# Attention block with a quantised side branch on one core: value products in two bursts, an opening that projects batch 2 early

## What is computed

```python
xn = layernorm(x)                                   # no weights
k, q, v = split(xn @ Wqkv + bqkv)                   # 16 heads of 16
scores = einsum('bsnh,btnh->bnst', k, q) / 4
scores = triu(scores) - 10000 * tril(ones, k=-1)
attn = softmax(scores, axis=2)
attn_out = einsum('bnkq,bknh->bqnh', attn, v) @ Wo + bo
x_fp8 = clip(xn / s, -448, 448).astype(float8_e4m3)  # s: input scale
ffn_out = (x_fp8 * s) @ (w_fp8 * w_scale).T
out = x + attn_out + ffn_out
```

## Time and profile before

| what | us |
|---|---|
| median of 3 executions | 215.1 (211.27 to 216.66) |
| the profiled execution: its own time | 213.12 |
| its span, first to last instruction | 211.4 |
| PE busy | 184.2 (87%) |
| DVE busy | 158.8 (75%) |
| POOL busy | 116.2 (55%) |
| ACT busy | 97.0 (46%) |

### The profile page before, as it was taken

The page is one execution under the profiler, slowest core; times in us unless marked ns, Lnnn a source line. Parts: engine busy times, 40 slices in busy tenths (PEclk is TensorE's granted clock), DMA queues, the critical chain, the costliest instruction groups (busy, mean ns, idle before and its releaser), DMA issues.

```text
span 211.4 us, 4667 instructions
## 1 busy us (share of the span) xinstructions
PE 184.2 (87%) x1677; PEld 137.4 (65%) x1677; DVE 158.8 (75%) x342; ACT 97.0 (46%) x169; POOL 116.2 (55%) x207
## 2 busy tenths in 40 slices
PE   4697564699979999999999999999999997997892
PEld 4586353567657677767776777777776764764561
DVE  2778979966778798969796979597959777970451
ACT  2514221236346633763366436643655455348510
POOL 6810600079963795369636973597359737635410
PEclk9999978569999999999999999999999999999998
DMA  5799986302610370137013621352136210001002
GB/s 178 171 333 207 210 203 184 72 2 79 175 51 7 102 200 6 56 88 201 22 50 81 168 60 53 81 150 80 54 81 167 63 50 2 3 5 50 3 3 99
DMA packets 23673, 20.35 MB, mean 96 GB/s; under 512 B 2547, under 2 KB 23395, under 8 KB 23651
## 3 DMA queue, kind: packets, MB, share of 16 engines
q1 hardware_dynamic: 23651, 20.06, 36.4%
HBM read 3.48 MB, written 2.10 MB: 26 GB/s over the span
## 4 chain that ended last, share of the span: by engine, by line
PE 66%; DVE 10%; SPq 9%; issue 5%; ACT 4%; DMA 3%; POOL 2%; ACTq 0%
PE pso L976 8%; PE bankB L1001 8%; SPq L356 7%; PE bankA L1001 7%; PE bankA L1063 6%; PE bankB L1009 5%; PE ps L951 5%; PE ps L956 4%; PE ps L928 3%; PE ps L930 2%; PE bankB L1030 2%; DVE o_masked L758 2%; DVE row_max L721 2%; PE pso L982 2%; PE bankB L1041 2%
## 5 line engine op out<-in xcount | busy, mean ns | idle before, releaser
L460 POOL TENSOR_SCALAR_AFFINE_SELECT probs<-probs 128x256 f32<-128x256 f32 x128 | 52.0, 436 | 70.1 <-ACT probs L525 70.1
L525 ACT ACTIVATE probs<-ps 128x1024 f32<-128x1024 f32 x48 | 49.1, 1025 | 37.2 <-PE ps L951 32.1
L721 DVE TENSOR_REDUCE row_max<-ps 128x4 f32<-128x1024 f32 (+1 forms) x48 | 58.1, 1216 | 2.4 <-PE ps L930 1.3
L951 PE MATMUL ps<-q_stack,k_stack 99*128 99x256 bf16 x128 | 20.0, 281 | 2.9 <-DMA q_stack<-max_rows 2.6
L976 PE MATMUL pso<-probs,v_sb 128*32 128x256 f32 x256 | 20.9, 398 | 0.5 <-POOL probs L460 0.3
L928 PE MATMUL ps<-k_stack,q_stack 96*128 96x128 bf16 x128 | 19.1, 226 | 2.0 <-DVE row_max L721 1.9
L1001 PE MATMUL bankB<-xT,wqk_sb 128*128 128x256 f32 x64 | 18.4, 438 | 1.7 <-ACT xT L575 1.7
L930 PE MATMUL ps<-k_stack,q_stack 125*128 125x128 bf16 x128 | 19.0, 225 | 0.0
L1001 PE MATMUL bankA<-xT,wqk_sb 128*128 128x256 f32 x64 | 16.8, 407 | 0.0
L1001 PEld LDWEIGHTS bankB<-xT,wqk_sb 128*128 128x128 f32 x64 | 13.2, 217 | 4.5 <-ACT xT L575 1.3
L1009 PE MATMUL bankB<-wqkv_sb,xT 128*128 128x256 f32 x64 | 15.3, 382 | 0.3 <-DVE q_rest L746 0.3
(11 more groups left out here) (130 smaller groups left out, 351.3 us busy)
## 6 DMA issues: line engine op xcount, KB each, us to landing
q_stack<-q_parts SPq DMA_DIRECT2D x48, 128.0 KB
k_stack<-k_parts SPq DMA_DIRECT2D x48, 128.0 KB
out_dram<-y SPq DMA_DIRECT2D x8, 256.0 KB, 2.1
x_all<-in_L_attn_x_dram SPq DMA_DIRECT2D x1, 1536.0 KB, 9.9
k_stack<-fixed_k SPq DMA_DIRECT2D x3, 256.0 KB
q_stack<-fixed_q SPq DMA_DIRECT2D x3, 256.0 KB
x_all<-in_L_attn_x_dram SPq DMA_DIRECT2D x2, 256.0 KB, 3.0
wqkv_sb<-in_L_attn_Wqkv_dram SPq DMA_DIRECT2D x1, 512.0 KB, 4.3
```

The source lines that it names most:

```text
L460: ins = pool.affine_select(out=v[:, lo:lo + 2], in_=v[:, lo:lo + 2], compare_op=ALU.is_ge, fill=0.0, base=0, pattern=[[0, 2], [1, P]], cha ...
L525: act.activation(probs[:, i % 2, :], ps[:], ACT.Exp, scale=SCALE).then_inc(exp_done, 1)
L721: dve.tensor_reduce(dst, src, AX_X, ALU.max).then_inc(max_done, 1)
L951: mm = pe.matmul(ps[:, h * S:h * S + S], k_stack[0:K_SOFT, b % STACKS, hh, 0:P], q_stack[0:K_SOFT, b % STACKS, hh, :], start=True, stop=True)
```

## The change

- Warm-up: 13 fp32 products instead of 18 transposes.
- x is loaded in four groups: batch 0, batch 1, batches 2 and 3, batches 4 to 7. The last is issued in step -1 behind the maxima rows, and so are the fixed rows of stack 2. Its statistics are taken in step 0 behind maximum 4, its square roots at the end of ACT's step 0, inverse_std(3) in step 1.
- Batch 2 is transposed and projected (q, k) in PE's step -1 between the maxima blocks of batch 0, v of batch 1 too; ACT does their copies before its steps, POOL splits batch 2 before its steps, SP lays it out in step 0. Step 0 no longer does this.
- On DVE, the magnitude half of clip_x becomes magnitude_x. In step 0 only that half stays for batch 0, in the later steps it moves behind maximum 2. fp8_weight and bv_T move into step -1 behind maximum 4, PE's weight transposes and bias product behind its last maxima block; the masked-key counts move into step 0.
- values: slots 0 to 2 of batch n are run together in slot 3 of step n, slots 3 to 5 together in slot 0 of step n+1 (the last batch keeps its order). probs has six slots, and exponentials waits for the value product six slots back. project_v stands before transpose_o, o_out(n, 0) behind values_out.
- split's subtraction, round_x and residual work in two pieces of 256 elements (split's for DVE too).

```diff
...
-USES_BEFORE = {"A": [("k", 0), ("k", 1)], "B": [("xT", 0), ("q", 0), ("xT", 1), ("q", 1), ("v", 0)]}
+USES_BEFORE = {"A": [("k", 0), ("k", 1), ("k", 2)],
+               "B": [("xT", 0), ("q", 0), ("xT", 1), ("q", 1), ("v", 0), ("xT", 2), ("q", 2), ("v", 1)]}
 FIRST, LAST = -1, B + 1
...
-        probs = sb("probs", [P, 2, 1024])
+        probs = sb("probs", [P, SLOTS, 1024])
...
-        WARM_UP = 18
+        WARM_UP = 13
         NEG = 4
         CONSTS = 3
-        X_GROUPS = ((0, TB), (TB, 2 * TB), (2 * TB, B * TB))
+        X_GROUPS = ((0, TB), (TB, 2 * TB), (2 * TB, 4 * TB), (4 * TB, B * TB))
...
             wait(eng, part2_ready, 2 * b + j + 1)
-            eng.tensor_tensor(pt[:, par, 2], r[:], pt[:, par, 1], ALU.subtract).then_inc(split_ready, 1)
+            for k in range(KT):
+                ins = eng.tensor_tensor(pt[:, par, 2, k], r[:, k], pt[:, par, 1, k], ALU.subtract)
+            ins.then_inc(split_ready, 1)
...
                     to_stack(n + 2)
+                if st.like == 0:
+                    to_stack(2)
                 if st.has(1):
                     max_to_stack(n + 1, 1 - p, 0)
+                if st.like == FIRST:
+                    load_x(3)
+                    fixed_in_stack(2)
             to_stack(1)
-            fixed_in_stack(2)
             all_steps(sp, run)
...
                 wait(pool, quant_dve, 4 * b + 4)
-                pool.tensor_tensor(x_sum[:], x_clip[:, par], x_big[:, par], ALU.add).then_inc(quant_pool, 1)
+                wait(pool, quant_pool, 2 * b)
+                for k in range(KT):
+                    ins = pool.tensor_tensor(x_sum[:, k], x_clip[:, par, k], x_big[:, par, k], ALU.add)
+                ins.then_inc(quant_pool, 1)
                 wait(pool, quant_pool, 2 * b + 1)
                 wait(pool, ffn_mm, b - 1)
-                pool.tensor_tensor(xq[:, par], x_sum[:], x_big[:, par], ALU.subtract).then_inc(quant_pool, 1)
+                for k in range(KT):
+                    ins = pool.tensor_tensor(xq[:, par, k], x_sum[:, k], x_big[:, par, k], ALU.subtract)
+                ins.then_inc(quant_pool, 1)
                 wait(pool, y1_ready, b)
-                pool.tensor_tensor(xb[:], x_all[:, TB * b:TB * b + TB, :],
-                                   out_bias[:].unsqueeze(1).to_broadcast([P, TB, D]),
-                                   ALU.add).then_inc(xb_ready, 1)
+                for g, (lo, _) in enumerate(X_GROUPS):
+                    if lo == TB * b:
+                        pool.wait_ge(x_landed[g], 16)
+                for t in range(TB):
+                    ins = pool.tensor_tensor(xb[:, t], x_all[:, TB * b + t, :], out_bias[:], ALU.add)
+                ins.then_inc(xb_ready, 1)
...
                         pool.wait_ge(out_bias_ready, 1)
-                        for g in range(3):
-                            pool.wait_ge(x_landed[g], 16)
                         residual(0)
...
             pool.wait_ge(split_ready, 2)
-            for qk in "qk":
-                split(pool, 1, 1, qk)
+            for b in range(1, 3):
+                for qk in "qk":
+                    split(pool, b, b % 2, qk)
             all_steps(pool, run)
...
                 act.wait_ge(ph2_mm, c + 1)
-                wait(act, pv_mm, c - 1)
+                wait(act, pv_mm, c - SLOTS + 1)
                 ps = ps1 if st.like == B - 1 and i % 2 else ps2
-                act.activation(probs[:, i % 2, :], ps[:], ACT.Exp, scale=SCALE).then_inc(exp_done, 1)
+                act.activation(probs[:, i, :], ps[:], ACT.Exp, scale=SCALE).then_inc(exp_done, 1)
...
                     exponentials(st, n, 3)
-                    o_out(n, 0)
                 if st.does("v"):
                 if st.has(0):
+                    o_out(n, 0)
                     exponentials(st, n, 4)
...
                     max_out(n + 1, 1 - p, 1, None)
+                if st.like == 0:
+                    square_roots(3)
...
                 part1(b, b, "k", "A")
+            square_roots(2)
             act.wait_ge(v_ones_ready, 1)
             values_out(0, 0)
-            square_roots(2)
+            xT_out(2, 0)
+            part1(2, 0, "q", "B")
+            part1(2, 0, "k", "A")
+            values_out(1, 1)
             all_steps(act, run)
...
                 dve.tensor_scalar(x_clip[:, par], x_over[:], -FP8_MAX, None, ALU.max).then_inc(quant_dve, 1)
+            def magnitude_x(b, par):
                 dve.wait_ge(quant_dve, 4 * b + 2)
...
                                   ALU.mult).then_inc(masked_ready, 1)
+            def count_masked_keys():
+                dve.wait_ge(const_ready, CONSTS)
+                link(dve.tensor_reduce(row_number[:], later[:], AX_X, ALU.add))
+                for t in range(TB):
+                    ins = dve.tensor_scalar(masked_keys[:, t:t + 1], row_number[:], -1.0, float(S - 1 - P * t), ALU.mult, ALU.add)
+                link(ins)
...
                     dve.tensor_tensor(out_bias[:], pso[:, 1, 0], bo_all[:], ALU.add).then_inc(out_bias_ready, 1)
-                    clip_x(0, 0)
+                    magnitude_x(0, 0)
+                    count_masked_keys()
                 if st.has(1):
                     maxima(st, n + 1, 1)
+                if st.like == FIRST:
+                    rest1(2, 0, "q", "B")
                 if st.has(1) and FIRST < st.like < EARLY:
...
                     clip_x(n + 1, 1 - p)
+                if st.has(1) and FIRST < st.like:
+                    magnitude_x(n + 1, 1 - p)
                 if st.does("xT"):
                     negate_and_split(n + 1, 0)
+                if st.like == FIRST:
+                    rest1(2, 0, "k", "A")
                 if st.has(-1):
...
                     maxima(st, n + 1, 4)
+                if st.like == FIRST:
+                    fp8_weight()
+                    dve.wait_ge(bias_mm, 1)
+                    dve.tensor_copy(bv_T[:], pso[:, 0, 0].rearrange("p (k m) -> p k m", k=KT)).then_inc(bv_T_ready, 1)
+                if st.like == 0:
+                    dve.wait_ge(x_landed[3], 16)
+                    link(moments(*X_GROUPS[3]))
+                    variances(3)
                 if st.has(0):
                     maxima(st, n + 1, 5)
-                if st.like == FIRST:
-                    inverse_std(2)
-                    normalise(2, 0)
+                if st.like == 1:
+                    inverse_std(3)
                 if st.like == EARLY:
...
             dve.wait_ge(bqk_col_ready, 1)
-            at, last = X_GROUPS[2]
             rest1(0, 0, "q", "B")
             split(dve, 0, 0, "k")
+            rest1(1, 1, "q", "B")
             dve.wait_ge(x_landed[2], 16)
-            moments(at, at + 5)
-            rest1(1, 1, "q", "B")
-            moments(at + 5, at + 8)
+            link(moments(*X_GROUPS[2]))
+            variances(2)
             rest1(1, 1, "k", "A")
-            fp8_weight()
-            dve.wait_ge(bias_mm, 1)
-            dve.tensor_copy(bv_T[:], pso[:, 0, 0].rearrange("p (k m) -> p k m", k=KT)).then_inc(bv_T_ready, 1)
-            link(moments(at + 8, last))
-            variances(2)
...
+            clip_x(0, 0)
+            inverse_std(2)
+            normalise(2, 0)
             dve.wait_ge(floor_ready, 1)
...
+            def transpose_w8():
...
             def bias_product():
...
             for _ in range(WARM_UP):
-                pe.transpose(ps1[:, 0:P], ident[:], ident[:])
+                pe.matmul(ps1[:, 0:P], ident[:], ident[:], start=True, stop=True)
             transpose_x(None, 0, 0)
...
-            pe.wait_ge(w8_ready, 1)
...
             pe.wait_ge(const_ready, CONSTS)
...
                         phase1(st, n + 1, 1 - p, i)
-                        if st.like == FIRST and i == 1:
-                            bias_product()
+                        if st.like == FIRST:
+                            if i == 0:
+                                transpose_x(None, 2, 0)
+                            elif i == 1:
+                                project_qk(None, 2, 0, "q", "B")
+                            elif i == 2:
+                                project_qk(None, 2, 0, "k", "A")
+                            elif i == 3:
+                                project_v(None, 1, 1)
+                            elif i == 5:
+                                transpose_w8()
+                                bias_product()
                         if i == (4 if st.like == FIRST else 5):
...
                             phase2(st, n, p, j)
-                    if i > 0 and st.has(0):
+                    if i > 0 and st.like == B - 1:
                         values(st, n, p, i - 1)
                     if i == 0 and st.has(-1):
-                        values(st, n - 1, 1 - p, SLOTS - 1)
+                        for j in range(SLOTS // 2, SLOTS):
+                            values(st, n - 1, 1 - p, j)
                     if i == 0:
...
                     elif i == 3:
+                        if st.does("v"):
```

(6 more changed lines are left out.)

23 lines of the change are left out of this document (10 added, 13 removed).

## The result

The kernel after the change takes 215.63 us (median of 4 runs, 215.11 to 216.31), the kernel before, run beside it on the same chip, 213.19 (210.97 to 216.66): ratio 1.0147, 95% interval 1.0099 to 1.0194. Forecast were 207 us, a range of 201 to 213, and faster with a chance of 0.77. The time is outside the range and on the other side of no change, though by less than 2%. Medians here are over all executions; the ratios leave out those, met with many of the kernels, that ran over 1.5% longer than the shortest of the same kernel. The profiled executions stand 2.0 us apart: 215.11 for 213.12, spans 213.4 for 211.4.

The account below looks back on a forecast made before the run. PE was taken to bound the plain steps and DVE step -1. The terms -2.3 (to step 1's start), -5.0 (bursts), +0.8 (table loads), -0.2 (steps 6 to 8) gave 206.4 us profiled, 208.3 median; said 207, range 201 to 213.

Parts of the forecast that it names:

- Warm-up: Opening: 13 fp32 products raise the clock for batch 0's q and k; k_parts of batch 0 comes 2.2 us earlier.
- I add up to 25.2: End of the opening: DVE's first maximum begins at 25.2 us for 28.82, -3.6.
- 8.1 + 1.8 + 1.5 + 1.8 - 0.6: Step -1 on DVE: old time, both rests, fp8_weight and bv_T, q_rest's wait, less old idle: 12.6 us, +4.5.
- fourth term: Step -1: new DVE wait for q_rest, behind transpose, copy, product and ACT, some 1.8 us.
- fifth: Step -1: DVE's old idle time of 0.6 us goes, -0.6.
- a term of 1.2 us for both steps: Steps -1 and 0: low clock costs 0 to 10 us; the half case was taken, +1.2.
- I keep 2.0: Step 0: of 6.2 us in which DVE was not busy 2.0 stay; with 17.5 busy, 19.5 for 23.8, -4.3.
- 0.7 + 0.47 + 0.2 - 0.35 = 1.0 a step: Steps 1 to 5: fewer groups, k_rest's wait gone, o_masked in time, less the wait for maximum 2; -5.0 in all.
- Table loads, +0.8: End of ACT's step 0: two table loads for group 3's square roots push xT of batch 3, +0.8 us.
- The opening gives nothing: Rival: statistics and projections only move, DVE ends step 0 as late as before; 208.7 us, chance 0.17.
- The slow rival: Steps -1 and 0: PE at 1.2 GHz, DVE waits for q, +9.3 for +1.2; 214.5 or 216.5 us, chance 0.07.
- The rival of the DVE-bound plain step: Plain steps: DVE becomes the bound, bursts give nothing, PE waits for maximum 2 and o_masked; 211.4 us, chance 0.17.

Follow-up runs that it names:

- after_filled: Kernel after the change, with products that nothing reads in PE's holes of the opening, step -1 and step 0: 214.19 us, ratio 1.0024.
- proj_only: Kernel after the change, with x in three groups again, all statistics before the maxima, early projections and new warm-up kept: 214.15 us, ratio 1.0058.
- bursts_256: Kernel after the change with its whole opening undone (bursts, mended order and POOL pieces on the kernel before): 210.75 us, ratio 0.9893.
- groups_only: bursts_256 plus x in four groups with the late stack rows and statistics, no early projections, old warm-up: 210.43 us, ratio 0.9875.
- after_512: Kernel after the change with POOL's pieces of 256 undone (split, round_x, residual whole again): 217.43 us, ratio 1.0192.
- before_bursts: Kernel before, with bursts, six probs slots and mended order, POOL whole, opening as before: 210.84 us, ratio 0.9875.

## Why the prediction was wrong, step by step

**Warm-up: right in the mechanism, worth nothing.** The q product of batch 0 took 1.97 us, as foreseen, with 5.0 us for the warm-up (forecast 3.2 to 6.1). But the clock is lost again in the next hole: 0.71 in 16:18, and the q product of batch 1 takes 3.05 us where it took 1.97. The forecast used the gain for batch 0 and took batch 1 as before; it looked for the next hole only behind 22 us.

**First maximum, "I add up to 25.2": 27.36.** The transfer did land earlier than foreseen, but DVE's queue ran late. It had waited 2.21 us for q_parts of batch 1 at 20.07, behind the product of 3.05 us, and has no gap to speak of from there on. The list behind k_rest of batch 1 (clip, inverse_std, normalise) was put at 2.7 us and took 3.5 (23.88 to 27.36). Small instructions were undersized in it: variances and inverse_std(2) have single instructions of 0.42, 0.47 and 0.59 us while POOL splits batch 1, where the shortest of their kind take 0.16.

**Step -1, "8.1 + 1.8 + 1.5 + 1.8 - 0.6": 15.00. Its fourth term failed by 1.5 us and its fifth by 0.9.** DVE's busy time grew by 3.2 (10.65 for 7.45), within 0.1 of what was added. The new wait for q_rest was set at 1.8, worked out with a product of 1.97 us; at the low clock it is 3.33. And "the old idle of 0.6 goes" was wrong: DVE waits 0.93 for maximum 1, since PE runs the transposes of batch 2 ahead of that block. The price of the low clock had been named ("q and k cost 1.8 us more each (3.75 for 1.97) and DVE waits for them") and was taken by half, in a term of 1.2 us for both steps. With the clock held high (after_filled) the step still took 14.0, with waits of 0.89 and 2.32: undersized by 1.4 us even at 2.4 GHz, less what the products that nothing reads take themselves.

**Step 0, 17.5 busy and "I keep 2.0": 18.31 and 3.3.** This is the step that misled most: that PE, losing 7 to 8 us of products, would free the step down to DVE's 17.5. DVE was indeed the bound, but then only its own work could shorten the step, and by the forecast's own count that hardly fell (17.64 to 17.5). What was left to gain were 6.2 us not busy, of which 3.3 stayed: 0.80 for the next block behind the transposes of w8, 1.18 for the ffn product, and 1.0 at the step's end for transpose_o (L1076), which gives o_sum. The PE work ahead of the second and in the third ran at 1.2 GHz (0.50 in 52:54 and 62:64). PE for its part stood still for 3.59 us before 61.97, waiting for o_masked, which stood behind the statistics in DVE's queue. The eight tiles of statistics are DVE work put into a step bound by DVE: with them step 0 is 2.6 us longer (21.60 for 18.99 in proj_only), for a first maximum that comes 1.8 us earlier.

**Bursts, "0.7 + 0.47 + 0.2 - 0.35 = 1.0 a step": 0.46 in step 3 (21.05 for 21.51), 1.5 us over steps 2 to 5.** The groups gave 0.51 of busy time, not 0.7, and the wait for k_rest of 0.47 did go. What failed is the sum: it treated the saving on PE and the waits as independent. PE's saving reaches the step's length only as far as DVE is ready, and the term of 0.2 for o_masked coming in time had the wrong sign (0.19 became 0.39, and 0.78 without the pieces), as DVE's whole queue moved later in the step. The forecast did name maximum 2 as the new wait (0.28 for the 0.35 said). For the groups, the Trainium skill (TensorEngine Tiling (Array Packing), Key Properties) says that a change of tiling mode drains the engine; the rows agree that a change costs something, 0.51 us over the four groups that went. For the pieces, "L755 would wait at most one half piece, -0.4" came out at 0.43 for 0.84 us; that the negate group would land beside POOL was not foreseen. The bursts also shorten step 0, by 1.2 us in bursts_256, which the forecast left out; so against a kernel with bursts and the old opening the new one starts step 1 4.3 us later (63.96 for 59.62), and not 3.2.

**Table loads, +0.8: about borne out.** The two loads took 1.28 us each. Step 1 is 0.8 longer than in proj_only, which has no such loads (23.09 for 22.33), but only 0.3 longer in groups_only than in bursts_256 (22.94 for 22.66); inverse_std(3) came in with them, PE's granted clock in the step is lower too (0.91 for 1.00), and no run has the loads alone. Rows of ACT's timeline after show how they lie.

```profile
64.39 1.28 ACT L532 ACT_TABLE_LOAD   x1
65.68 0.21 ACT L532 ACTIVATE std<-var_eps 128x8 f32<-128x8 f32 x1
65.91 1.28 ACT L539 ACT_TABLE_LOAD   x1
```

The Trainium skill (ScalarE: Activation LUTs, What ACT_TABLE_LOAD costs) adds a drain of 1380 ns to a switch. The trace doesn't agree: the square root starts 0.01 us after the load ends, and the next load 0.02 after the square root; the 2.8 us more that the page would have cost didn't come.

**The rivals.** None holds alone. "The opening gives nothing" was nearest in its place (208.7, with full bursts). The slow rival had the place right, q's chain in DVE's queue at the low clock, and its time (216.5) is the nearest to the measured 215.63, but this is in part luck: it put all of the loss on the clock and kept the full bursts. With the clock up in step -1 the kernel is at 214.19 us, 1.4 under 215.63 by the medians and 2.6 by the ratios (1.0024 for 1.0147), where the opening missed its forecast by 5.5. The rival of the DVE-bound plain step was half right (PE does wait for row_max and o_masked, 0.28 and 0.39, at 21.05 a step and not 21.3). What was missing is one case in which the opening loses and the bursts give half; each was priced alone, and the chance of both was not.

**What remains open.** Why single value products cost PE 0.35 us more busy time with the mended order than without (21.19 for 20.85) wasn't looked into. Whether early projections could pay with less of DVE's other work in step -1 wasn't tried. Why one and the same opening takes up to 1.8 us more in one profiled execution than in another (step 1 at 57.86, 58.06 and 59.62 us in the three kernels with bursts and the old opening, which differ only in order and pieces) stays open too. The fastest kernels measured are those with the change but without its early projections, at 210.4 to 210.8 us with or without the x groups and the pieces; their own difference is below what was measured.

## What to carry to other kernels

Moving products off a busy TensorE stretch gains only if the engine that ends that stretch loses work too: cut the trace at both stretches, and compare the busy time of the engine whose instructions form the chain, not that of PE. An instruction that moves into an in-order queue takes its longest input chain with it; price that wait at the lower clock when PE has just been idle. And edits to the order and to the grouping of the same queue are no sum: here one gave 0.11 us, the other -0.94, and both 0.27.

## What the runs showed of the hardware that wasn't expected

- The granted clock rose for the first product after 13 fp32 products of the identity (q in 1.97 us; 3.75 after 18 transposes) and fell in the sparse microseconds behind it, so that the next batch's q took 3.05. After the 3.61 us hole before 27.50 it was at 1.2 GHz (0.50 in 28:30 and 30:32) though PE was busy throughout, and a q product took 3.75.
- Three value products in a row cost 0.48 us each for 0.57 singly. Over six a step PE's busy time fell by 0.51 us.
- Instructions of 16 columns on DVE, 0.16 to 0.17 us by themselves, took 0.55 to 0.59 while POOL ran an instruction of split (L303, subtracting 256 columns, or L300, scaling 512); with the subtraction whole, 512 columns, one of them took 1.04 (after_512, before_bursts). Cutting POOL's instructions shortened the longest and spread the wait over more of them: the four took 0.55, 0.59, 0.16 and 0.55 for 1.04, 0.54, 0.16 and 0.17 in after_512, about the same in all.
